# The place of the dense products among the attention work in a two-layer decoder kernel's second layer

## The reference

```python
def attention(q, k, v, mask):                     # 16 heads of 32
    scores = einsum('bhqd,bhkd->bhqk', q, k) / sqrt(32)
    scores = scores * mask - 10000.0 * (1.0 - mask)
    return einsum('bhqk,bhkd->bhqd', softmax(scores), v)

q, k, v = split(layernorm(x, ln1_s, ln1_b) @ w_qkv + b_qkv, 3)
x = x + merge(attention(q, k, v, ltor_mask)) @ w_ao + b_ao        # "self" round
q = layernorm(x, ln2_s, ln2_b) @ w_q + b_q
k, v = split(encoder_states @ w_kv + b_kv, 2)
x = x + merge(attention(q, k, v, cross_mask)) @ w_co + b_co       # "cross" round
x = x + gelu(layernorm(x, ln3_s, ln3_b) @ w1 + b1) @ w2 + b2      # the network
```

## Time and profile before

| | |
|---|---|
| median of three runs | 1841.54 us |
| profiled execution | 1842.27 us, span 1840.5 us |
| TensorE busy, of the span | 93% |
| VectorE, ScalarE, GpSimd busy | 66%, 58%, 8% |
| TensorE's granted clock, mean | 0.959 |
| the second layer's attentions | from about 758 to 1450 us |

### The profile page before, as it was taken

The page is one execution under the profiler, slowest core; times in us unless marked ns, Lnnn a source line. Parts: engine busy times, 40 slices in busy tenths (PEclk is TensorE's granted clock), DMA queues, the critical chain, the costliest instruction groups (busy, mean ns, idle before and its releaser), DMA issues.

```text
span 1840.5 us, 32546 instructions
## 1 busy us (share of the span) xinstructions
PE 1717.6 (93%) x11840; PEld 1233.4 (67%) x11840; DVE 1207.0 (66%) x2792; ACT 1060.4 (58%) x2333; POOL 142.4 (8%) x207
## 2 busy tenths in 40 slices
PE   3879999999999988999999999999999899999999
PEld 2424343444434333788889888888888789999998
DVE  5666776767776552588888888888888663333332
ACT  2345666756666564587788777777777631111111
POOL 2110101101000000000000000100000100000000
PEclk8779999999999898999999989999999999999999
DMA  6322223222222222567557757666666330000000
GB/s 161 111 86 67 94 82 100 71 93 88 83 71 68 80 61 87 152 157 182 153 156 200 198 163 200 169 173 173 167 167 168 116 121 25 25 25 25 25 26 13
DMA packets 169479, 201.62 MB, mean 110 GB/s; under 512 B 25956, under 2 KB 117220, under 8 KB 169320
## 3 DMA queue, kind: packets, MB, share of 16 engines
q1 hardware_dynamic: 169032, 199.14, 38.5%
q10 hardware_dynamic: 288, 0.39, 0.2%
HBM read 131.84 MB, written 67.63 MB: 108 GB/s over the span
## 4 chain that ended last, share of the span: by engine, by line
PE 81%; DVE 9%; ACT 5%; issue 2%; DVEq 1%; DMA 1%; ACTq 0%; POOL 0%; SPq 0%
PE c_d L2121 10%; PE b_d L1379 10%; PE c_sums L2136 10%; PE b_d L1391 9%; PE a_d L499 6%; PE b_d L1458 5%; PE a_escore L472 5%; PE a_d L569 3%; PE a_d L577 3%; PE a_mscore L484 3%; PE a_d L553 3%; PE b_score L1446 3%; PE b_d L1475 3%; DVE a_mx L802 2%; PE a_d L561 2%
## 5 line engine op out<-in xcount | busy, mean ns | idle before, releaser
L802 DVE TENSOR_REDUCE a_mx<-a_mscore 128x2 f32<-128x1024 f32 x247 | 302.3, 1224 | 171.8 <-PE a_mscore L484 170.2
L639 ACT ACTIVATE a_pt<-a_escore 128x1024 f32<-128x1024 f32 x256 | 262.5, 1025 | 165.1 <-PE a_escore L472 164.9
L1605 ACT ACTIVATE b_pr<-b_t,b_nmax 128x256 f32<-128x256 f32 x512 | 254.5, 501 | 121.4 <-DVE b_nmax L1781 121.0
L2220 ACT ACTIVATE c_gT<-c_d,c_b 128x256 f32<-128x256 f32 x128 | 53.7, 472 | 267.4 <-PE c_d L2121 267.4
L1777 DVE TENSOR_TENSOR b_t<-b_score,b_mask 128x1024 f32<-128x1024 f32 x128 | 155.0, 1211 | 75.6 <-PE b_score L1446 75.6
L1781 DVE CUSTOM_DVE_ANT_0 b_t<-b_t,b_minus 128x256 f32<-128x256 f32 x512 | 191.1, 429 | 16.9
L472 PEld LDWEIGHTS a_escore<-a_qst,a_kst 50*128 50x128 f32 x512 | 50.0, 191 | 180.4 <-ACT a_pt L639 109.6
L472 PE MATMUL a_escore<-a_qst,a_kst 50*128 50x512 f32 x512 | 133.8, 518 | 24.2 <-ACT a_pt L639 23.7
L2265 DVE CAST c_g_high<-c_gT 128x512 fp32r<-128x512 f32 x64 | 38.1, 595 | 172.0 <-ACT c_gT L2220 172.0
L2121 PE MATMUL c_d<-c_ln_high,c_w_high 128*128 128x256 f32 x512 | 145.4, 284 | 2.4 <-DVE c_ln_low L2267 2.4
L2121 PE MATMUL c_d<-c_ln_high,c_w_low 128*128 128x256 f32 x512 | 145.6, 284 | 0.0
(11 more groups left out here) (166 smaller groups left out, 3255.5 us busy)
## 6 DMA issues: line engine op xcount, KB each, us to landing
b_qst<-b_q SPq DMA_DIRECT2D x96, 256.0 KB, 4.7
b_kst<-b_k SPq DMA_DIRECT2D x96, 256.0 KB, 6.4
b_q<-b_qparts SPq DMA_DIRECT2D x64, 256.0 KB, 4.5
b_k<-b_kparts SPq DMA_DIRECT2D x64, 256.0 KB, 3.6
a_qst<-a_q_parts SPq DMA_DIRECT2D x192, 64.0 KB, 2.2
a_kst<-a_k_parts SPq DMA_DIRECT2D x186, 64.0 KB, 2.2
a_k_parts<-a_kparts SPq DMA_DIRECT2D x32, 256.0 KB, 2.3
a_q_parts<-a_qparts SPq DMA_DIRECT2D x32, 256.0 KB, 2.3
```

What stands on the lines that cost most here:

```text
L639: nc.scalar.activation(pt[:, at % RING, :, :], escore[:], ACT.Exp, scale=SCALE).then_inc(exp_done.sem, 1)
L802: nc.vector.tensor_reduce(mx[:, 2 * pair:2 * pair + 2, q], maxima_bank(b, n)[:], AX_X, ALU.max).then_inc(max_done.sem, 1)
L1605: last = nc.scalar.activation(pr[:, u % 2, j, :], t[:, u % 2, j, :], ACT.Exp, scale=-1.0, bias=nmax[:, u, j:j + 1], accum_out=esum[:, u, j ...
```

## The change

In `position` of TensorE's queue, `fill` goes from the end of a position to the place right behind the scores, ahead of the transposes of the probabilities and of the weighing. The list `uses` follows it, so that the banks are handed round in the new order. The queues of the other engines stay as they are.

```diff
@@ uses, the order of the banks
         for v in range(LAST + 1):
             for p in range(NU):
+                uses += [(name, v + shift, n) for name, n, shift in FILL[p] if has(name, v + shift)]
                 w, u = unit_at(v, p)
                 if there(w):
                     uses += [("pt", w, u * TT + k) for k in range(TT)]
                 if p % 2 == 0:
                     w, u = unit_at(v, p - 2)
                     if there(w):
                         uses += [("w", w, u // 2)]
-                uses += [(name, v + shift, n) for name, n, shift in FILL[p] if has(name, v + shift)]
@@ TensorE
             def position(v, p):
                 scores(*unit_at(v, p + 2))
+                fill(v, p)
                 turn_probs(*unit_at(v, p))
                 if p % 2 == 0:
                     w, u = unit_at(v, p - 2)
                     weigh(w, u // 2)
-                fill(v, p)
```

## The result

The changed kernel takes 1974.21 us (median of four runs, 1973.17 to 1978.15) against 1841.07 us (median of four runs of the kernel before): 1.0724 times the time before, 95% interval 1.0707 to 1.0741. 1971 was forecast, in a range of 1915 to 2020.

A forecast was written before the change was run, and what follows sets the result against it. The prediction took TensorE as the bound, VectorE and ScalarE following closely. The profiled 1842.3 us plus 113 of waits over the rounds plus 16.5 for the clock, less 0.7, gave 1971 us, range 1915 to 2020.

The forecast's parts named there:

- The bound and the mechanism: Second layer: TensorE bounds, VectorE and ScalarE close behind; each bank use waits for the reader of the use six places before.
- the list of predecessors: Each use's bank predecessor in both orders; named new waits in positions 0, 1, 2, 4, 5, 6 and 7.
- Positions of a cross round: Rounds 6 to 13: added 0.25, 1.15, 1.45, 0.5, 4.6, -0.2 and 1.15 us in positions 0, 1, 2, 4, 5, 6, 7; 8.9 together.
- A self round: Rounds 1 to 5: added waits of 0.25+1.15+1.45+0.5+1.95+1.15 = 6.45 us a round, 32.3 in all.
- The clock: TensorE's clock falls behind waits: 13 x 1.5 + 4 x 1.5 - 9 = 16.5 us added.
- the third case: The clock paragraph's pointer to its extreme, where the clock falls at every wait: 2024 us.
- case 2: Rival: TensorE's clock falls at every wait, 1841.5+113+69 = 2024 us; chance 0.12.
- Rounds with weights: Rounds 6 and 8, where VectorE splits weights: 4 us more; round 0, without weighing and output products yet: 2 us.
- The round times foretold: Changed profile: cross rounds of 52 to 54 us for 43.5, self rounds of 47 to 48.5 for 40.5.
- Case 1: Rival: queues absorb the small waits, only o0's bank is late, clock about even: 1887 us; chance 0.13.
- Case 3: Rival: position 6's wait goes, nothing replaces it, 1821 us; needs residual_sum(0) done by 1.3 us into position 5; chance 0.05.
- Case 4: Rival: TensorE's stream bounds and the order is of no account, 1841.5 us; chance 0.02.

The follow-up runs named there:

- e1: TensorE's queue as after the change, banks handed round in the old list, against the kernel before: 1943.83 us, 1.0563.
- e2: TensorE's queue as before the change, banks handed round in the new list, against the kernel before: 2217.81 us, 1.2052.
- e3: New TensorE queue, each use given the bank read out earliest, round 14 back on the list, against the kernel before: 1836.0 us, 0.998.
- e6: As e3, but round 14 also chooses banks by read-out and the opening's q0 and k0 are due at 1.0; against the kernel before: 1828.52 us, 0.9938.
- e5: Kernel after the change with VectorE's residual sum of o0 moved ahead of softening in position 5; against the kernel before: 1916.26 us, 1.041.
- e7: Old TensorE queue, banks by earliest read-out, round 14 included and the opening's q0 and k0 due at 1.0; against the kernel before: 1819.9 us, 0.9886.

## Why the prediction was right, step by step

- **The bound and the mechanism** held. Taking either half of the diff back changes which waits there are, in the places that the list of predecessors names (e1, e2), and choosing banks by read-out takes them away with the new queue in place, but for one in round 6 (e3, e6). The kernel after and e6 have the same queues and differ only in the banks: 1974 and 1829 us.
- **Positions of a cross round**, worked out and measured in round 11 or 12: position 0 5.85 and 5.73; 1 and 7 5.37 and 5.26; 2 6.96 and 6.92; 3 4.92 and 4.97; 4 6.6 and 6.5; 5, without what the low clock adds, 9.8 and 9.7; 6 7.6 (7.8 less 0.2) and 7.4. VectorE is free of the dividing 1.21 us after the scores, where 1.24 was worked out. Most single terms are about 0.1 too high: in the kernel after, TensorE starts 0.06 us behind the residual sum's end (1209.44+0.68 against 1210.18) where I had 0.1 to 0.2. The wait for o0's bank is 4.20 and not 4.6, since the idle time is counted from the end of "enc", 1.6 us after the scores, and not from 1.28.
- **A self round**: 6.45 worked out, 5.9 measured. Position 5 was put at 6.3 and is 6.21; the rest is position 4, 6.50 us, which costs 0.3 to 0.4 over the 6.1 to 6.2 that four of the five rounds had before and nothing over round 1's 6.6, and position 0, 0.14 for 0.25.
- **The clock** was about right in sum and wrong in place. I put 1.5 us into each of 13 rounds and 1.5 more into half of the cross rounds, 25.5 us. The self rounds after have none: their waits of up to 1.7 us leave the granted clock at 1.00. The cross rounds have 1.8 to 2.6 us each in position 5, 19.3 in all. More of it stands in rounds 0 and 15, where none was put: the query projection of position 6 in round 0 takes 4.36 us, the first output product in round 15 5.21 for 3.08. That the sum comes near is luck. The prediction's pointer from this paragraph to "the third case" is a slip: it means case 2. The two windows below, rounds 1 to 5 and 9 to 13 with their neighbours, show it: stretch, length, busy us of each engine, granted clock, share of DMA, GB/s.

```profile
820.00:1050.00 230.00, 204.57 (x1917) 179.74 (x1915) 171.55 (x544) 162.34 (x491) 15.84 (x45) 1.00 0.59 153
1175.00:1500.00 325.00, 267.10 (x2325) 231.56 (x2326) 218.49 (x671) 200.24 (x598) 18.62 (x52) 0.93 0.53 142
```

- **Rounds with weights** were put too low: rounds 6 to 8 cost 38.5 us, where three cross rounds, the 4 us on top and their share of the clock's 16.5 (1.3 us in each of 13 rounds) had 34.5; round 0 cost 5.6 for 2. The trace names waits there that full rounds don't have, such as 7.93 us for o0's bank and 5.41 us for line 1752 in round 6. The prediction had no row for work queued ahead of these readers but the 2.47 us of the earlier trace rows. Round 15, put at nothing, has 5.6 us from its first scores on: the list is in force there too, and the second half of position 5's transposes waits 2.33 us for o0's bank. The rest is mostly low clock, in position 4 (8.39 us for 7.27) and behind this wait:

```profile
1573.21 1.73 PE L1458 MATMUL b_d<-b_ident,b_pr 128*128 128x128 f32 x12 [2.33 <-DVE b_xr L1819]
```

So the closeness of 1971 to 1974 is in part luck. Rounds 1 to 5 were put 9.2 us too high, 38.6 with their share of the clock for 29.4 measured, and round 14 1.5 too high; round 0, rounds 6 to 8 and round 15 were put 3.6, 4.0 and 5.6 too low. Only rounds 9 to 13 came out by themselves, 50.8 us for 51.3. The round times foretold, 47 to 48.5 us for self rounds and 52 to 54 for cross rounds, were missed a little on either side, with 46.5 to 46.8 and, in rounds 9 to 13, 54.2 to 55.2.

- **The rivals.** Case 1 (only o0's bank is late, 1887) fails at the 55 us of waits for line 1752; e5, in which o0's wait is nearly gone, still takes 1916. Case 2 (the clock falls at every wait, 2024) fails at the self rounds' granted clock of 1.00. Case 3 (faster) failed at its own condition: residual_sum(0) ends at 5.7 us into position 5, not 1.3. Case 4 (the order is of no account) fails at the 133 us. The Trainium skill, "Perfetto Trace Analysis", section "Matmuls", says that independent matmul groups should rotate through different PSUM banks. The kernel before (1841), the kernel after (1974), e2 (2218) and e7 (1820) all do so; in these runs the time depends on which bank comes next.

## What to carry to other kernels

With banks handed out in a fixed rotation, moving a group in the producer's queue moves its bank's reader in front of another group: before such a move, list for each use who read its bank last and when. If the readers' order is known, hand a use the bank that is read out first, not the one of n uses ago; here that gave 1.1% with no instruction changed. And a reader that someone waits for belongs ahead of its engine's long work of the position, if what it pushes back isn't waited for: the residual sum moved ahead gave 58 us, and cost 1.0 us in each self round where line 1728 came late by it.

## What the runs showed of the hardware

TensorE's clock falls behind some waits, and the length of the wait alone doesn't say how much is lost.

- Waits of 0.8, 1.4 to 1.7 us, several in every 46 us, cost nothing in rounds 1 to 5 of the kernel after (granted clock 1.00 from 820 to 1050 us).
- Before the change, behind waits of 2.06 us, the query projection took 4.60 us in every second of rounds 8 to 13 (granted clock 0.63 in that of the earlier trace rows, from 1152.5 to 1157.1 us) and 3.10 us in the others (1.00 from 1197.8 to 1200.9).
- In e1, behind waits of 2.8 us, the output product lost 2.7 or 1.6 us, mostly by turns (granted clock 0.50 and 0.64 in the two shown).
- The waits of 4.2 us of the kernel after cost the output product 2.1 to 2.6 us in rounds 7 to 13, and the one of 7.9 us in round 6 cost 1.8.

Why waits of one length are followed by different losses was not settled by these runs.
